# Filler matmuls at the end of routing, the first tiles read by ScalarE, spare tiles that read pads, and three stage changes in a fused state-space, attention and expert kernel

## The chip, the cores and the metric

The kernel runs on one core of one Trainium2 chip. The metric is the device time of one execution in microseconds (us); the time of the kernel before is the median of three runs.

## The reference

Eight batches of 768 tokens with 256 features. The first 256 tokens of a batch (the image) come out of a state-space kernel, the other 512 (the text) are an input. Attention with 16 query and 4 key/value heads of 64 features follows, then a router that sends each token to the 2 best of 8 experts, all in float32:

```
h = tok(log_dt, inv_A_real, A_imag, B_ri, x)         # (8, 256, 256)
h = concatenate([h, txt], axis=1)                    # (8, 768, 256)
h = h + attention(layernorm(h), Wq, Wk, Wv, Wo)      # rotary, softmax, 16 heads on 4
h = h + ffn(layernorm(h), Wr, br, W1, b1, W2, b2)
# ffn: logits = x @ Wr + br; the two largest, softmax over the two;
#      gate * (relu(x @ W1[e] + b1[e]) @ W2[e] + b2[e]), summed over the two experts
```

## The kernel before

There are three blocks of instructions, one after the other; each engine has its own queue in a block and works in order, and semaphores tie the queues together.

**The state-space block** (`vandermonde`) builds powers of a complex number on VectorE, multiplies four banks on TensorE (line 197), lets ScalarE copy each bank out (L171), and stores the image rows of batch 0 to DRAM (L143). The block ends when these stores have landed.

**The attention block** starts with a hand-written order of work for batch 0. SyncE loads the image rows and the text rows of batch 0 (L516, L517) and stores the image rows of the other seven batches (L614). VectorE takes the statistics of all six tiles of 128 tokens (L496, L500), refines the inverse root in small chained instructions (L485 to L504) and normalises four tiles (L850); GpSimd normalises two (L781). TensorE then runs the list `FIRST`: three transposing jobs (L633), four key jobs, four query jobs and four more query jobs for the next group of heads (L642); ScalarE copies each result out of PSUM (L713, L719, L717). VectorE applies the rotary turn to keys and queries in `rotate`, 6 instructions a half (L470, L474, L475). SyncE moves the keys and then, in 16 DMAs, the queries (L622), and the loop over 8 batches and 4 groups of heads begins with the score matmuls (L656) and the maxima (L812).

**The third block** holds `route` and `experts`. In `route`, a batch is six calls of `project` (8 matmuls of 256 columns each, L980), and between them stand, for the batch before, `turn` (12 transposes, L988), `logits` (12 matmuls of 8 columns, L996) and `counts` (L1003, L1004). TensorE's three banks `A[:, t % 3]` are read by VectorE's `add` (L1078). VectorE normalises the batch (`norm`, up to L1103), picks the experts (`choose`, from L1110 to L1125), and gives each pair of token and expert a row (`place`, up to L1149). GpSimd then writes the rows to `xs_d` with 12 indirect DMAs a batch (L963). The last batch has nothing beside it: TensorE's `drain` is `turn`, `logits`, `counts`. After `place`, VectorE writes `tail_i` (L1163), from which SyncE and ScalarE put 128 pad rows behind each expert's rows (L934, L1066), and `tile_table` (L1190 to L1212) works out for each of 103 tiles its expert, the row that it starts at (`src_i`) and for how many earlier output DMAs its own has to wait (`adds_i`). The table has room for more tiles than the data fill. A tile past the last real one reads the last real tile again and has a gate of zero, and `adds_i` makes its output DMA wait for the one before.

In `experts`, SyncE loads the rows and the first weights of four tiles ahead (L1258, L1262). Before the first rows it waits for all scatters, pads and stores. A tile is two transposes (L1292), 8 matmuls up (L1302), a relu on ScalarE (L1340), 4 matmuls down (L1309), bias and gate on VectorE (L1382, L1384), and an indirect DMA on GpSimd that adds the rows to the output in DRAM (L1365); rows with an index beyond the last token are skipped.

## Time and profile before

| what | value |
|---|---|
| time of three runs | 2265.6 to 2272.73 us, median 2267.47 |
| the profiled execution | 2265.04 us, span 2263.3 us |
| busy: TensorE, VectorE, ScalarE, GpSimd | 2047.4, 1770.0, 1072.6, 879.4 us |
| mean granted TensorE clock | 0.959 of 2.4 GHz |

Busy times are sums over the whole span, and the stages have different limits, so the table only says that TensorE is busy for nine tenths of it. What an edit is worth is read from the stage that it touches. The profiled execution spends 1.74 us outside its span and is 2.43 us below the median.

### The profile page before, as it was taken

Reading aid. Unit: us, or ns where it says so; the run is one execution under the profiler, and the core shown is the slowest. Engines: PE = TensorE matmul, PEld = TensorE weight load, DVE = VectorE, ACT = ScalarE, POOL = GpSimd, SP = SyncE. Lnnn points to the kernel's source line nnn. Section 1 sums busy time; section 2 is a strip of 40 time slices with the busy share of each in tenths; the row PEclk is TensorE's granted clock in tenths of the full one; section 3 lists DMA queues with packets and bytes.
Section 4 is the critical chain, followed back from the end, with each engine's and each line's share of the span. In section 5 each row is a group of like instructions: output and inputs, shape, how many; then the busy total and the mean of one; then the engine's idle time right before and its main releaser. Section 6 shows DMA issues by size and latency. Waiting matters only on the chain. (4 is left out here: it accounts for less than half of the span.)

```text
span 2263.3 us, 59177 instructions
## 1 busy us (share of the span) xinstructions
PE 2047.4 (90%) x21098; PEld 1237.6 (55%) x21099; DVE 1770.0 (78%) x3212; ACT 1072.6 (47%) x2463; POOL 879.4 (39%) x833
## 2 busy tenths in 40 slices
PE   0369999999999999999999999997899949999997
PEld 0234444444444444444444445443588839999996
DVE  8769999999999999999999999999144544444443
ACT  2035655655556555655665565555021114444442
POOL 0023454264344542642444436221034443444443
PEclk6689999999999999999999999999899969999998
DMA  2143543634544445435444453453677648898885
GB/s 51 43 107 90 136 118 92 159 106 103 142 113 126 117 107 137 116 108 128 120 120 120 102 133 105 117 131 95 202 258 269 216 136 212 210 212 209 215 210 117
DMA packets 189542, 317.28 MB, mean 140 GB/s; under 512 B 48661, under 2 KB 127121, under 8 KB 189329
## 3 DMA queue, kind: packets, MB, share of 16 engines
q1 hardware_dynamic: 156640, 275.39, 45.1%
q0 software_dynamic: 19440, 25.83, 6.2%
q10 hardware_dynamic: 13248, 13.13, 1.7%
q8 instruction: 144, 2.36, 0.5%
q14 instruction: 70, 0.57, 0.1%
HBM read 214.75 MB, written 92.31 MB: 136 GB/s over the span
## 5 line engine op out<-in xcount | busy, mean ns | idle before, releaser
L725 ACT ACTIVATE a_prob<-ps_s,a_nmax 128x768 f32<-128x768 f32 x768 | 686.3, 898 | 578.9 <-DVE a_nmax L812 578.9
L812 DVE TENSOR_REDUCE a_nmax<-ps_s 128x1 f32<-128x768 f32 x768 | 694.1, 943 | 49.4 <-PE ps_s L656 44.2
L818 DVE STREAM_TRANSPOSE a_probT<-a_prob 128x768 f32<-128x768 f32 x768 | 700.0, 949 | 1.4 <-PE ps_o L663 1.4
L656 PE MATMUL ps_s<-a_kT,a_qT 64*128 64x384 f32 x3072 | 614.7, 514 | 54.7 <-ACT a_prob L725 50.8
L663 PE MATMUL ps_o<-a_probT,a_vrep 32*64 32x384 f32 x12288 | 561.2, 491 | 6.8 <-DVE a_probT L818 5.0
L656 PEld LDWEIGHTS ps_s<-a_kT,a_qT 64*128 64x128 f32 x3072 | 259.7, 186 | 391.5 <-ACT a_prob L725 275.3
L788 POOL TENSOR_TENSOR a_o<-a_o,a_invrow 128x1536 f32<-128x1536 f32 x32 | 110.0, 3437 | 791.0 <-ACT a_o L733 791.0
L663 PEld LDWEIGHTS ps_o<-a_probT,a_vrep 32*64 32x64 f32 x12288 | 243.6, 132 | 293.8 <-issue 129.9
L470 POOL TENSOR_TENSOR a_prod<-a_raw,a_table 128x384 f32<-128x384 f32 x304 | 294.5, 1002 | 29.1 <-DVE a_qp L475 22.1
L1365 POOL DMA_INDIRECT out_dram<-e_y,e_row_i x103 | 160.6, 1559 | 239.9 <-DMA out_dram<-e_y,e_row_i 138.6
L1302 PE MATMUL ps_r<-e_xT,e_w 128*128 128x128 f32 x1648 | 201.8, 276 | 0.0
L1309 PE MATMUL ps_r<-ew,e_hT 128*128 x824 | 194.7, 379 | 0.0
L1302 PEld LDWEIGHTS ps_r<-e_xT,e_w 128*128 128x128 f32 x1648 | 193.3, 193 | 0.1
L1340 ACT ACTIVATE e_hT<-ps_r,e_b_now 128x128 f32<-128x128 f32 x412 | 117.8, 368 | 158.9 <-PE ps_r L1302 100.0
L980 PE MATMUL ps_r<-wo,r_oT 128*128 128x256 f32 x768 | 180.9, 397 | 9.7 <-POOL base L945 9.7
L642 PE MATMUL ps_o<-a_xT,wq 128*128 128x384 f32 x512 | 185.8, 501 | 0.0
L980 PEld LDWEIGHTS ps_r<-wo,r_oT 128*128 128x128 f32 x768 | 151.5, 200 | 32.2 <-POOL base L945 10.4
L1309 PEld LDWEIGHTS ps_r<-ew,e_hT 128*128 128x128 f32 x824 | 148.8, 190 | 16.0
L963 POOL DMA_INDIRECT xs_d<-r_xn,r_idx x96 | 93.8, 977 | 150.1 <-DVE h L1078 119.1
L725 ACT ACTIVATION_READ_ACCUMULATOR a_prob<-ps_s,a_nmax 128x1 f32 x768 | 151.0, 197 | 0.0
L642 PEld LDWEIGHTS ps_o<-a_xT,wq 128*128 128x128 f32 x512 | 91.0, 189 | 88.9 <-issue 25.6
L1382 DVE TENSOR_TENSOR e_y<-ps_r,eb 128x256 f32<-128x256 f32 x103 | 43.7, 424 | 99.9 <-PE ps_r L1309 97.9
(211 smaller groups left out, 1291.5 us busy)
## 6 DMA issues: line engine op xcount, KB each, us to landing
e_w<-in_L_ffn_W_dram SPq DMA_DIRECT2D x103, 512.0 KB, 4.3
a_qT<-q_d SPq DMA_DIRECT2D x124, 384.0 KB, 8.9
a_vrep<-v_d SPq DMA_DIRECT2D x128, 192.0 KB, 3.8
a_invrow<-inv_d SPq DMA_DIRECT2D x64, 384.0 KB, 5.1
oT_d<-a_o SPq DMA_DIRECT2D x32, 768.0 KB, 3.3
r_oT<-oT_d SPq DMA_DIRECT2D x64, 384.0 KB, 8.4
q_d<-a_qp SPq DMA_DIRECT2D x31, 768.0 KB, 3.7
e_x<-xs_d SPq DMA_DIRECT2D x103, 132.0 KB, 3.6
```

What stands on the lines that cost most here:

```text
L470: eng.tensor_tensor(scratch[n], a, f, ALU.mult).then_inc(done, 1)
L642: last = pe.matmul(X[:, 0:HALF], w, xn[:, k, HALF * c:HALF * c + HALF], start=(k == 0), stop=(k == KC - 1))
L656: last = pe.matmul(S[:, s % 2, r, 0:HALF], qT[rows, par, 2 * hp + c, P * t:P * t + P], kT[rows, par, :], start=True, stop=True)
L663: last = pe.matmul(O[DH * c:DH * c + DH, q, 0:HALF], vrep[rows, j % NQ, j // NQ, :], keys(par, c, j, rows), start=(j == 0), stop=(j == NJ ...
L725: act.activation(prob[:, s % RING, :].rearrange("p (r k) -> p r k", r=2), S[:, s % 2, :, 0:HALF], ACT.Exp, bias=nmax[:, s % RING:s % RING ...
L812: v.tensor_reduce(nmax[:, s % RING:s % RING + 1], S[:, s % 2, :, 0:HALF], AX.XY, ALU.max, negate=True).then_inc(max_ready, 1)
L818: v.transpose(turned(par, s), prob[:, s % RING, :]).then_inc(t_ready, 1)
L980: last = pe.matmul(A[:, t % 3, 0:D], oT[:, q, c // 2, c % 2, P * t:P * t + P], wo[:, c, :], start=(c == 0), stop=(c == KV * 2 - 1))
L1302: last = pe.matmul(H[:, q, P * f:P * f + P], w1[:, n, c, P * f:P * f + P], xT[:, q, P * c:P * c + P], start=(c == 0), stop=(c == KC - 1))
L1309: last = pe.matmul(Y[:, q, 0:D], hT[:, q, P * c:P * c + P], w2[:, bass.ds(ex, 1), c, :], start=(c == 0), stop=(c == FC - 1))
L1340: last = act.activation(hT[:, q, P * f:P * f + P], H[:, q, P * f:P * f + P], ACT.Relu, bias=b1_now[:, n, f:f + 1], scale=1.0)
L1365: pool.indirect_dma_start(out=acc_d, out_offset=bass.IndirectOffsetOnAxis(ap=row_i[:, n:n + 1], axis=0), in_=y[:, n, :], in_offset=None, c ...
```

## The change

- **State-space and attention.** The text rows of batch 0 are loaded and normalised within the state-space block (`normalise_rows` on VectorE, after the last of its products). The attention block only loads and normalises the image rows, all on VectorE. `FIRST` starts with the text rows, and the halves of keys and queries that hold only text come first. VectorE's first turns use the buffer `prod`, and they stand before its wait for the stored rows.
- **Routing.** The logits of a batch are put between the matmuls of the third `project` of the next, two matmuls behind each of its last six. TensorE no longer waits for four constants at the start.
- **The end of routing.** `warm(n)` issues n matmuls of 256 columns into a bank that nobody reads; 106 of them are put around the last batch's work and behind it, with waits for `tail_ready` and `table_ready` between.
- **The tile table and the first tiles.** Spare tiles start at the pads behind the last expert's rows, and do not wait for one another. `needs_i` holds for the first 8 tiles whether they need the last batch's rows. ScalarE issues the first four row loads, as soon as the table is there and `placed` has the value that the tile needs; SyncE issues all four first weights at once. GpSimd waits for the stores of the residual before its first output DMA.

```
+def normalise_rows(v, k, x, ln, tiles):
+
+    st, mv, ve, y, y2 = ln
+    some = slice(tiles[0], tiles[-1] + 1)
+    for t in tiles:
+        k.mark(v.bn_stats(st[:, t, :], x[:, t, :]))
+    v.wait_ge(k.sem, k.base + k.n)
+    for t in tiles:
+        k.mark(v.bn_aggr(mv[:, t, :], st[:, t, :]))
+    v.wait_ge(k.sem, k.base + k.n)
+    k.link(v.tensor_scalar(ve[:, some], mv[:, some, 1], EPS, None, ALU.add))
+    k.link(v.tensor_scalar(y[:, some].bitcast(I32), ve[:, some].bitcast(I32), 1, None, ALU.arith_shift_right))
+    k.link(v.tensor_scalar(y[:, some].bitcast(I32), y[:, some].bitcast(I32), -1.0, float(0x5f3759df), ALU.mult, ALU.add))
+    for _ in range(3):
+        k.link(v.tensor_tensor(y2[:, some], y[:, some], y[:, some], ALU.mult))
+        k.link(v.tensor_tensor(y2[:, some], y2[:, some], ve[:, some], ALU.mult))
+        k.link(v.tensor_scalar(y2[:, some], y2[:, some], -0.5, 1.5, ALU.mult, ALU.add))
+        k.link(v.tensor_tensor(y[:, some], y[:, some], y2[:, some], ALU.mult))
+    for t in tiles:
+        last = v.tensor_scalar(x[:, t, :], x[:, t, :], mv[:, t, 0:1], y[:, t:t + 1], ALU.subtract, ALU.mult)
+    return last
+
...
+                sp.dma_start(x0[:, IT:TT, :], io["txt"][0].rearrange("(t p) d -> p t d", p=P)).then_inc(x_in, 16)
...
                     v.wait_ge(g_ready, q + 1)
+                v.wait_ge(x_in, 16)
+                normalise_rows(v, Tally(v, text_dve), x0, ln, range(IT, TT)).then_inc(text_ready, 1)
...
-    FIRST = N_JOBS + K_JOBS + Q_JOBS + Q_JOBS
-    FIRST_AT = {"n": 0, "k": 3, "q": 7, "q1": 11}
+    FIRST = [("text", 0, 0), ("text", 1, 0), ("k", 1, 0), ("k", 1, 1), ("image", 0, 0), ("k", 0, 0), ("k", 0, 1),
+             ("q", 1, 0), ("q", 1, 1), ("q", 0, 0), ("q", 0, 1)] + Q_JOBS
+    IMAGE_AT = FIRST.index(("image", 0, 0))
+    FIRST_AT = {"q1": 11}
...
                 def iteration(b, g):
                     i = b * KV + g
                     if first_it(i):
-                        hold(sp, x_done, len(N_JOBS))
+                        hold(sp, x_done, IMAGE_AT + 1)
...
 
...
                 for c in range(1, NB):
                     sp.dma_start(token_rows(img_d, c), kt[c:P:NB]).then_inc(rows_stored, 16)
-                hold(sp, part["k"], 2 * LINKS)
-                move_k(0, 0)
+                for r in (1, 0):
+                    hold(sp, part["k"], (2 - r) * LINKS)
+                    for h in range(2):
+                        at = DH * r + HH * h
+                        sp.dma_start(kT[at:at + HH, 0, :], kp[0:HH, h, HALF * r:HALF * r + HALF]).then_inc(k_in[0], 16)
...
 
-                    if job == "n":
+                    if job == "text":
+                        for m in range(TT - IT):
+                            last = pe.transpose(X[:, P * m:P * m + P], x[:, IT + m, P * c:P * c + P], ident[:])
+                    elif job == "image":
+                        for m in range(4):
+                            last = pe.transpose(X[:, P * m:P * m + P], x[:, m % IT, P * (m // IT):P * (m // IT) + P], ident[:])
+                    elif job == "n":
...
                     for n in range(NJ // GROUP):
                         group(NB - 1, KV, n)
 
-                pe.wait_ge(norm_ready, 1)
-                pe.wait_ge(norm_first, 1)
+                pe.wait_ge(text_ready, 1)
                 pe.wait_ge(loaded, LOADED)
                 for n, (job, c, h) in enumerate(FIRST):
-                    wait(pe, x_out, len(N_JOBS) if n == len(N_JOBS) else n - NQ + 1)
+                    if n == IMAGE_AT:
+                        pe.wait_ge(norm_ready, 1)
+                    wait(pe, x_out, n if n in (2, IMAGE_AT + 1) else n - NQ + 1)
...
-                    free = (part["q"], (c + 1) * LINKS) if n >= FIRST_AT["q1"] and h == 0 else None
+                    free = (part["q"], (2 - c) * LINKS) if n >= FIRST_AT["q1"] and h == 0 else None
                     evacuate(O[:, n % NQ], n, job, c, h, free)
                 loop(act, iteration, drain)
 
...
 
                 def normalise(n):
-                    if n > 0:
-                        for at in range(3, 6):
-                            stats(pool, n, at)
+                    for at in range(3, 6):
+                        stats(pool, n, at)
                     hold(pool, norm_dve, n * NORMS + NORMS)
-                    for t in range(TT if n else ON_POOL):
+                    for t in range(TT):
                         last = pool.tensor_scalar(x[:, t, :], x[:, t, :], mv[:, t, 0:1], y[:, t:t + 1], ALU.subtract, ALU.mult)
                     last.then_inc(norm_ready, 1)
 
...
                         scale_o(i - 1)
 
-                normalise(0)
...
-                for at in range(6):
-                    stats(v, 0, at)
-                v.wait_ge(norm_dve, NORMS)
-                for t in range(ON_POOL, TT):
-                    last = v.tensor_scalar(x[:, t, :], x[:, t, :], mv[:, t, 0:1], y[:, t:t + 1], ALU.subtract, ALU.mult)
-                last.then_inc(norm_first, 1)
+                v.wait_ge(x_in, 32)
+                k = Tally(v, norm_dve)
+                normalise_rows(v, k, x, ln, range(IT)).then_inc(norm_ready, 1)
+                v.nop().then_inc(norm_dve, NORMS - k.n)
                 v.memset(inv[:], 1.0).then_inc(set_ready, 1)
                 v.wait_ge(set_ready, 1)
                 v.wait_ge(table_in, 16)
+                for job, c, number in (("k", 1, 0), ("k", 0, 1), ("q", 1, 0), ("q", 0, 1)):
+                    rotate(v, job, c, number, [prod[:, n, :] for n in range(4)], FIRST.index((job, c, 1)) + 1, [])
                 v.wait_ge(rows_stored, (NB - 1) * 16)
-                flat = probT[:].rearrange("p a b q -> p (a b q)")
-                for job in "kq":
-                    for c in range(2):
-                        rotate(v, job, c, c, [flat[:, HALF * n:HALF * n + HALF] for n in range(4)], FIRST_AT[job] + 2 * c + 2, [])
                 loop(v, iteration, drain)
 
 
...
                     pool.indirect_dma_start(out=xs_d, out_offset=bass.IndirectOffsetOnAxis(ap=idx[:, q, e, t:t + 1], axis=0),
                                             in_=xn[:, q, t, :], in_offset=None).then_inc(scattered[q], 16)
             pool.wait_ge(scattered[q], k * (TT * TOPK * 16) + TT * TOPK * 16)
-            pool.nop().then_inc(xn_free, 1)
+            if isinstance(b, int) and b >= NB - 2:
+                if b == NB - 1:
+                    for r in range(2):
+                        pool.wait_ge(zeroed[r], 16 * (NE // 2))
+                pool.nop().then_inc(placed, 1)
+            else:
+                pool.nop().then_inc(xn_free, 1)
...
-        def project(b, q, t):
+        def project(b, q, t, beside=None):
             pe.wait_ge(oT_in[2 * q + t // 3], (b >> 1) * (KV * 16) + KV * 16)
             pe.wait_ge(h1_ready, b * TT + t + 1)
             for c in range(KV * 2):
                 last = pe.matmul(A[:, t % 3, 0:D], oT[:, q, c // 2, c % 2, P * t:P * t + P], wo[:, c, :], start=(c == 0), stop=(c == KV * 2 - 1))
+                if beside is not None and c >= KV * 2 - TT:
+                    logits(beside, [c - (KV * 2 - TT)])
             last.then_inc(oT_free, 1)
 
...
-        def logits(b):
-            pe.wait_ge(xT_ready, b * 3 + 3)
-            pe.wait_ge(mask_ready, b + 1)
-            for t in range(TT):
+        def logits(b, tiles):
+            if 0 in tiles:
+                pe.wait_ge(xT_ready, b * 3 + 3)
+                pe.wait_ge(mask_ready, b + 1)
+            for t in tiles:
                 for c in range(KC):
                     last = pe.matmul(L[:, NE * t:NE * t + NE], xT[:, c, P * t:P * t + P], wr[:, c, :], start=(c == 0), stop=(c == KC - 1))
-            last.then_inc(lg_done, 1)
+            if TT - 1 in tiles:
+                last.then_inc(lg_done, 1)
 
         def counts(b):
+            pe.wait_ge(const, 2)
             pe.wait_ge(mask_ready, b + 2)
             pe.wait_ge(idx_ready, b + 1)
...
-                project(b, q, t)
+                project(b, q, t, b - 1 if not first(b) and t == LOGITS_AT else None)
                 if not first(b) and t == TURN_AT:
                     turn(b - 1, 1 - q)
-                if not first(b) and t == LOGITS_AT:
-                    logits(b - 1)
                 if not first(b) and t == COUNTS_AT:
                     counts(b - 1)
 
+        def warm(count):
+            for _ in range(count):
+                pe.matmul(A[:, TT % 3, 0:D], ident[:], wo[:, 0, :], start=True, stop=True)
+
         def drain():
+            pe.wait_ge(h1_ready, NB * TT + 1)
+            warm(26)
             turn(NB - 1, 1)
-            logits(NB - 1)
+            warm(4)
+            logits(NB - 1, range(TT))
+            warm(12)
             counts(NB - 1)
-
-        pe.wait_ge(const, 4)
+            warm(20)
+            pe.wait_ge(tail_ready, 1)
+            warm(32)
+            pe.wait_ge(table_ready, 1)
+            warm(12)
+
         pe.wait_ge(wo_in, 16)
         loop(iteration, drain, pe)
...
             v.tensor_copy(tail_i[:], run[:]).then_inc(tail_ready, 1)
+            k = Tally(v, needs_dve)
+            k.link(v.tensor_scalar(full[:], off[:, 0, 0:1], 1.0 / P, -1.0, ALU.mult, ALU.add))
+            k.link(v.tensor_scalar(needs_i[:], tile_no[:, 0:AHEAD], full[:], 1.0, ALU.is_gt, ALU.add))
             tile_table(v, sb, table_dve, run, base, tile_no, pairs, exp_i, src_i, held_by, adds_i, table_ready).then_inc(adds_ready, 1)
...
     link(v.tensor_copy(end[:, 0:1], cnt[:, 0:1]))
-    for x in range(1, NE):
+    for x in range(1, NE - 1):
         link(v.tensor_tensor(end[:, x:x + 1], end[:, x - 1:x], cnt[:, x:x + 1], ALU.add))
-    link(v.tensor_scalar(last[:], end[:, NE - 1:NE], -1.0, None, ALU.add))
-    link(v.tensor_scalar(jr[:], j[:], last[:], None, ALU.min))
     shape = [P, NT, NE - 1]
-    link(v.tensor_tensor(past[:], jr[:].unsqueeze(2).to_broadcast(shape), end[:, 0:NE - 1].unsqueeze(1).to_broadcast(shape), ALU.is_ge))
+    link(v.tensor_tensor(past[:], j[:].unsqueeze(2).to_broadcast(shape), end[:, 0:NE - 1].unsqueeze(1).to_broadcast(shape), ALU.is_ge))
     link(v.tensor_reduce(e[:], past[:], AX.X, ALU.add))
     link(v.tensor_tensor(past[:], past[:], cnt[:, 0:NE - 1].unsqueeze(1).to_broadcast(shape), ALU.mult))
     link(v.tensor_reduce(start[:], past[:], AX.X, ALU.add))
-    link(v.tensor_tensor(start[:], jr[:], start[:], ALU.subtract))
+    link(v.tensor_tensor(start[:], j[:], start[:], ALU.subtract))
     link(v.tensor_scalar(start[:], start[:], float(P), None, ALU.mult))
     mark(v.tensor_copy(exp_i[:], e[:]))
-    link(v.tensor_scalar(ind[:], j[:], last[:], None, ALU.is_gt))
-    mark(v.scalar_tensor_tensor(out=held_by[:], in0=ind[:], scalar=-2.0 * NE, in1=e[:], op0=ALU.mult, op1=ALU.add))
-    v.scalar_tensor_tensor(out=src_i[:], in0=e[:], scalar=float(STRIDE), in1=start[:], op0=ALU.mult, op1=ALU.add).then_inc(rows_ready, 1)
+    mark(v.tensor_copy(held_by[:], e[:]))
+    link(v.scalar_tensor_tensor(out=start[:], in0=e[:], scalar=float(STRIDE), in1=start[:], op0=ALU.mult, op1=ALU.add))
+    v.tensor_scalar(src_i[:], start[:], run[:, NE - 1:NE], None, ALU.min).then_inc(rows_ready, 1)
     link(v.tensor_tensor(turn[:, 1:NT], e[:, 1:NT], e[:, 0:NT - 1], ALU.is_gt))
-    link(v.tensor_tensor(turn[:, 1:NT], turn[:, 1:NT], ind[:, 1:NT], ALU.max))
     return v.scalar_tensor_tensor(out=adds_i[:, 1:NT], in0=turn[:, 1:NT], scalar=16.0, in1=pairs[:, 1:NT], op0=ALU.mult, op1=ALU.add)
...
         def load(j, n):
+            if isinstance(j, int) and j < AHEAD:
+                needs = sp.value_load(at(needs_i, j), min_val=1, max_val=2)
+                hold(sp, placed, needs)
             row = sp.value_load(at(src_i, j), min_val=0, max_val=SLOTS - P)
             sp.dma_start(x[:, n, :], xs_d[bass.ds(row, P), :]).then_inc(x_in[n], 16)
 
@@ -1261,13 +1321,7 @@
             ex = sp.value_load(at(exp_i, j), min_val=0, max_val=NE - 1)
             sp.dma_start(w1[:, n], io["W1"][bass.ds(ex, 1)].rearrange("o (c p) f -> p (o c) f", p=P)).then_inc(w1_in[n], 16)
 
-        for n in range(2):
-            load_w1(n, n)
-        for s, value in landed:
-            sp.wait_ge(s, value)
         for n in range(RING):
-            load(n, n)
-        for n in range(2, RING):
             load_w1(n, n)
...
@@ -1277,6 +1331,8 @@
                 load(j + RING, n)
                 hold(sp, h_done, j + 1)
                 load_w1(j + RING, n)
+            if isinstance(j, int) and j == AHEAD - RING - 1:
+                sp.wait_ge(placed, 2)
 
...
+        act.wait_ge(table_ready, 1)
+        for n in range(RING):
+            needs = act.value_load(at(needs_i, n), min_val=1, max_val=2)
+            hold(act, placed, needs)
+            row = act.value_load(at(src_i, n), min_val=0, max_val=SLOTS - P)
+            act.dma_start(x[:, n, :], xs_d[bass.ds(row, P), :]).then_inc(x_in[n], 16)
         copy_x(0, 0)
         loop(act, tile)
...
         pool.wait_ge(adds_ready, 1)
+        pool.wait_ge(h_stored, 16 * NB)
         loop(pool, tile)
```

`AHEAD` is 8. `placed` is raised by GpSimd when the scatters of the last batch but one have landed, and again when those of the last batch and all pads have.

## Rows read from the trace of the kernel before

**Rows 1.** The page: span, and the granted clock in 40 slices (tenths).

```profile
span 2263.3 us, 59177 instructions
PEclk6689999999999999999999999999899969999998
```

**Rows 2.** Timeline, VectorE around the first block border: start, duration, instruction, idle before.

```profile
108.94 2.06 DVE L496 BATCH_NORM_STATS2 a_st<-a_x 128x6 f32<-128x256 f32 x6 [15.88 <-DMA a_x<-in_txt_dram]
...
111.58 0.17 DVE L502 TENSOR_SCALAR a_ve<-a_mv 128x6 f32<-128x6 f32 x1
...
114.75 1.61 DVE L850 TENSOR_SCALAR a_x<-a_x,a_mv,a_y 128x256 f32<-128x256 f32 x4
...
127.15 1.96 DVE L470 TENSOR_TENSOR a_probT<-a_raw,a_table 128x384 f32<-128x384 f32 x4 [10.75 <-ACT a_raw L719]
...
138.81 0.55 DVE L475 TENSOR_TENSOR a_qp<-a_probT 128x384 f32<-128x384 f32 x1
```

**Rows 3.** Timeline, SyncE's queue: loads of batch 0, moves of its queries.

```profile
104.54 0.38 SPq L516 DMA_DIRECT2D a_x<-img_d  x1
...
139.43 10.97 SPq L622 DMA_DIRECT2D a_qT<-a_qp  x16
```

**Rows 4.** DMA issues, 100 to 145 us: size and median us to landing.

```profile
a_x<-img_d SPq DMA_DIRECT2D x1, 256.0 KB, 2.7
```

**Rows 5.** Timeline, ScalarE's copies of the first two key jobs.

```profile
123.97 0.49 ACT L719 ACTIVATE a_raw<-ps_o 128x384 f32<-128x384 f32 x1 [3.02 <-PE ps_o L642]
126.53 0.49 ACT L719 ACTIVATE a_raw<-ps_o 128x384 f32<-128x384 f32 x1 [2.07 <-PE ps_o L642]
```

**Rows 6.** Timeline, TensorE's first transposes and first scores.

```profile
117.50 2.82 PE L633 MATMUL ps_o<-ident,a_x 128*128 128x128 f32 x12 [17.04 <-POOL a_x L781]
...
143.54 2.66 PE L656 MATMUL ps_s<-a_kT,a_qT 64*128 64x384 f32 x8 [3.94 <-DMA a_qT<-a_qp]
```

**Rows 7.** The chain of waits, two batches of routing: start, duration, piece.

```profile
1672.45 2.58 PE ps_r L996 x24
1675.03 3.56 PE ps_r L980 x16
...
1694.16 3.46 PE ps_r L980 x16
...
1700.19 5.24 PE ps_r L980 x16
```

**Rows 8.** Stretches: length; busy PE, PEld, DVE, ACT, POOL; granted clock; DMA.

```profile
1700.00:1705.00 5.00, 5.00 (x17) 4.13 (x17) 2.42 (x24) 1.49 (x2) 0.96 (x1) 0.66 1.10 372
...
1855.00:1860.00 5.00, 0.00 (x0) 0.00 (x0) 0.00 (x0) 0.00 (x0) 0.96 (x1) 0.50 0.23 78
```

**Rows 9.** Timeline, the last batch's routing and the first tile.

```profile
1824.24 2.82 PE L988 MATMUL ps_r<-ident,r_xn 128*128 128x128 f32 x12 [5.75 <-DVE r_xn L1103]
...
1833.07 0.21 DVE L1110 TENSOR_TENSOR r_lg<-ps_r,br 128x48 f32<-128x48 f32 x1 [8.89 <-PE ps_r L996]
...
1835.77 0.67 PE L1003 MATMUL ps_r<-r_mask,r_below 128*128 128x48 f32 x2 [2.74 <-DVE r_mask L1124]
...
1839.17 0.17 DVE L1149 CAST r_idx<-r_posf 128x12 uint32<-128x12 f32 x1
...
1847.53 0.26 DVE L1209 SCALAR_TENSOR_TENSOR src_i<-t_e,t_start 128x103 int32<-128x103 f32 x1
...
1860.62 0.69 PE L1292 MATMUL ps_r<-ident,e_x 128*128 128x128 f32 x2 [23.76 <-DMA e_x<-xs_d]
...
1868.88 1.95 PE L1302 MATMUL ps_r<-e_xT,e_w 128*128 128x128 f32 x16
```

**Rows 10.** Timeline, the last output DMAs and the last tile's result.

```profile
2236.76 1.55 POOL L1365 DMA_INDIRECT out_dram<-e_y,e_row_i  x1 [2.05 <-DVE e_y L1384]
...
2248.16 0.35 DVE L1384 TENSOR_SCALAR e_y<-e_y,e_gate 128x256 f32<-128x256 f32 x1
...
2255.17 1.55 POOL L1365 DMA_INDIRECT out_dram<-e_y,e_row_i  x1 [2.98 <-DMA out_dram<-e_y,e_row_i]
```

More of the change, by code:

```diff
@@ L1184, in tile_table @@
     ni = sb("t_ni", [P, NE], I32)
[L1185 to L1186 removed]
+    e, start, turn = (sb(f"t_{x}", [P, NT]) for x in ("e", "start", "turn"))
     past = sb("t_past", [P, NT, NE - 1])
```

47 lines of the change are left out of this document (27 added, 20 removed).

## The prediction

> **What bounds the kernel now.** I read the page first. Its row of the granted clock is full almost everywhere, and the slices below it are the first three, slice 29, where routing starts, and slice 33, where routing ends [rows 1]. In between lies the attention loop, about 1,450 us of a fixed pipeline. No part of the change touches it, so what is gained ahead of it arrives whole at the end. Next I read the timeline at three places that the diff touches. At the first block border VectorE is idle for 15.88 us for the text rows, and the queries' moves start only when its last rotary turn has ended [rows 2, 3]. In routing the chain of waits runs on TensorE alone. At the end of routing TensorE waits for everybody, at a granted clock of 0.50 [rows 8, 9]. In the expert loop TensorE is the bound again, and at the very end GpSimd's output DMAs are [rows 10].
>
> **Part 1, start of attention.** The text rows' statistics and four normalised tiles move into VectorE's idle time behind its last product. That is 2.06 us of statistics and 1.61 us of scaling for at least as many tiles, with some 3.2 us of small instructions between, under 7 us in 15.88 us of idle time, and the block border before the image load at 104.54 comes after it [rows 2, 3]. It costs nothing; without that cover it would be 7 us. The image rows land 2.7 us after 104.54, at 107.2 [rows 3, 4]. VectorE then needs two tiles of six (0.7 us of statistics, 0.2 of aggregation), the same small chain of 3.17 us (111.58 to 114.75), and two scalings (0.8): ready at 112.2, where TensorE began at 117.50 [rows 2, 6]. TensorE has transposed the text by 107.2 and done both key jobs of the second half by 112.3, at 2.56 us a job on the low clock [rows 5]. The image's transposes and copy take some 1.6 us more, to 113.9. The next two key jobs end at 116.5 if the clock has risen (half of 2.56 each) and at 119.0 if not, and are copied 0.7 us later. From there VectorE has three rotary turns of 3.05 us in a row (the four before run from 127.15 to 139.36) [rows 2]. They end at 126.4 or 128.9, in place of 139.36. That is 13.0 or 10.4 us; I take 12, because TensorE has by then worked for 7 us with one pause. What stands behind it, the moves of the queries and 4 us later the first scores, follows at the same distance [rows 3, 6]. GpSimd loses its two tiles. The first turns now use `prod`, which GpSimd takes over only after both query turns, as before. The seven stores of image rows are issued from the same time on.
>
> **Part 2, logits between the project's matmuls.** The matmuls are the same. A pass of a logit matmul is as long as its weight load (2.58 us for 24), a project pass as long as its 256 columns (3.46 us for 16) [rows 7]. The order does not change that sum, so the interleaving by itself is worth nothing. But behind five of seven logit stretches the next project takes 5.24 us in place of 3.56, and the clock over that stretch is 0.66 [rows 7, 8]. It fell after 2.58 us in which only 8 columns followed each weight load. With a project matmul before each pair, no such stretch is left. If the clock then holds, five times 1.68 is 8.4 us. VectorE's add of the third tile comes 2.3 us later and delays the choice of experts by some 0.5 us; the next to need it is `counts` behind the fourth project, which has about that much slack. The price is between 0 and 1 us in all; I take 0, and bound the gain at 0 and 8.4. The constants that TensorE no longer waits for I count at nothing, since the block border holds it too.
>
> **Part 3, the end of routing.** A filler is a float32 matmul of 256 columns with a weight load, the shape of a project matmul. Eight of these are 16 records in 3.46 us, so one is two passes and 0.433 us [rows 7]. The 106 fillers therefore hold TensorE for 45.9 us at the full clock. Before, from the end of the projects (1824.24 less 5.75, 1818.49) to the first tile's transposes at 1860.62 were 42.1 us [rows 9]. The fillers do not give way, so I add up TensorE's queue:
> 26 fillers, 11.2 us, to 1829.7 (the normalised batch has been there since 1824.2);
> `turn` 1.45 us (half of its 2.82 and a little), 4 fillers 1.7, `logits` 2.58, to 1835.5;
> 12 fillers, 5.2, to 1840.7 (the mask is ready 2.7 us after the logits, at 1838.2);
> `counts` 0.4, to 1841.1; the indices came 3.57 us after it started, some 3.1 on the full clock, so at 1843.8, where it was 1839.34 [rows 9].
> Then 20, 32 and 12 fillers, 27.7 us, to 1868.8. Neither wait holds them. `tail_ready` comes at 1843.8, and the table, 8.45 us from index to `src_i` before, has two instructions of 0.2 us more and six fewer, 7.7 us in sum, to 1851.5. ScalarE's row loads need about 1.5 us to issue and 2.7 to 4.3 to land, by 1857; even behind the whole old chain of scatters and pads, shifted by 4.5 us, they would be there by 1865.2. So the first transposes start at 1868.8, not at 1860.62: 8.2 us late. The full clock in the first tiles gives some 1.6 us back (0.69 us of transposes and a first tile's matmuls at half speed; bounds 0 and 2.5). The sum of this part is a loss of 6.6 us. The loads by ScalarE, the early weights and the shorter table are hidden behind the fillers. The wait for stores ahead of GpSimd's first output DMA is met long before its first tile, and SyncE's two more register loads a tile lie in a ring of four tiles.
> The Trainium skill (TensorE: Matmul & The Clock Gate, Back-to-back issue gap) gives 262 cycles for a matmul of 256 columns, 0.109 us at 2.4 GHz. By it the fillers would be 11.6 us and no delay at all. This case's row has four times that for float32, and the row decides.
>
> **Part 4, spare tiles.** The last four output DMAs each wait for the one before: from 2236.76 to 2255.17 is four steps of 4.60 us, while the last tile's result was there at 2248.5 [rows 10]. Now a DMA waits for the one two before it. The last can issue at about 2249.8 (0.95 us after its result, or 1.9 us after its neighbour), 5.4 us earlier. A DMA whose rows are all skipped may land sooner; nothing shows it, and it can give between 0 and the 3.7 us to landing. I take 0.
>
> **The sum.** 12.0 + 8.4 + 5.4 - 6.6 is 19.2 us. From the span of 2263.3 that is 2244.1; with the 1.74 us around it, 2245.8. The median of the runs lies 2.4 us above the profiled execution, so 2248 us against 2267.47.
>
> **The rivals.**
> *The clock still falls (18%).* Transposes and logits remain short streams, and a few low stretches stay or move. For it: the clock fell five times of seven here [rows 7, 8]. Against: the project's long passes now stand in every microsecond of it. All 8.4 us lost gives 2257.
> *The start doesn't matter (10%).* Something with a time of its own, such as the stores of the other seven batches, holds the first scores or the first loop. Against: the scores follow the moves by 4 us and end the wait [rows 3, 6]. The 12 us gone gives 2260; this part would then not do what it says.
> *Fillers are cheap (10%).* If a filler is one pass, 0.216 us, the 106 are 22.9 us. The turn is not delayed, the logits come at 1830.0, the table at 1843, the rows at 1847.8, and the first transposes some 12.8 us earlier than before, with the 1.6 us a gain of 14.4. That gives 2227. Against it stand 16 records for 8 matmuls. The page named above speaks for it.
> *Slower (5%).* The fillers run on the low clock. Each then costs 0.865 us, another 45.9 us for all of them: 2294. The batch before ends at the full clock and nothing idles between, which speaks against it. It decides for slower once 60 of the 106 are slow (26 us over 0.433).
>
> **How the numbers follow.** The forecast has the remaining 57%. Its own range is 2242 to 2254: 10.4 to 13 us at the start, 6.7 to 8.4 of clock, 4.5 to 7.5 at the end, a loss of 5 to 8 in the middle. The range takes in the first two rivals and leaves out cheap and slow fillers, 15%: 2238 to 2261. A change under 0.3% (6.8 us) is about what a measurement of this kernel cannot tell from none. The slow fillers are slower (5%), the upper ends of the first two rivals lie within 0.3% (5%), and all else, 90%, is faster.
>
> **What would show it.** First scores at 131 to 134 us. Project pieces behind the logits of 3.5 us, and no slice at 0.66 in routing. Fillers with two records each and 0.43 us; the last batch's turn some 11 us after its projects; no idle time of TensorE before the first tile's transposes, 50 us after the projects, with rows in place 10 us earlier. Output DMAs at the end 3.7 us apart or less. The forecast fails if fillers are not two passes, if the clock is not held, or if the first loop waits for something else.

## The result, and the profile after

The changed kernel took 2275.82 us (median of 20 runs, 2265.15 to 2291.12), the kernel before 2266.15 us (20 runs, 2262.59 to 2272.73): a ratio of 1.0045, 95% interval 1.003 to 1.006. It was slower by 9.7 us where 2248 was forecast. The profiled execution of it is the longest of the 20, so its rows overstate the typical run; but they show where the time is. One of the six runs of `fillers_fit` below (4234.83 us) and one of the eleven of before beside it (2502.28 us) were in a slow state; the medians include them, the ratios leave them out. The page, span and granted clock, for [rows 1]:

```profile
span 2289.3 us, 59644 instructions
PEclk6579999999999999999999999998978999999999
```

Timeline of the changed kernel, VectorE and TensorE at the start, for [rows 2, 6] (start, duration, instruction, idle before):

```profile
98.16 1.38 DVE L94 TENSOR_SCALAR a_x<-a_x,a_mv,a_y 128x256 f32<-128x256 f32 x4
107.88 0.75 DVE L80 BATCH_NORM_STATS2 a_st<-a_x 128x6 f32<-128x256 f32 x2 [8.34 <-DMA a_x<-img_d]
...
131.61 2.93 PE L693 MATMUL ps_s<-a_kT,a_qT 64*128 64x384 f32 x8 [3.64 <-DMA a_qT<-a_qp]
```

The text rows are normalised in idle time, and the first scores start at 131.61 where they started at 143.54 [rows 6]: 11.9 us, as forecast. Now the middle of routing, a stretch for which [rows 7] showed 3.56 us of project behind a block of logits. Timeline of one batch:

```profile
1687.81 0.40 ACTq L1100 DMA_DIRECT2D out_dram<-h  x1
...
1692.23 1.47 PE L1033 MATMUL ps_r<-ident,r_xn 128*128 128x128 f32 x12
...
1695.27 0.60 ACT L1092 ACTIVATE r_xT<-ps_r 128x512 f32<-128x512 f32 x1 [7.49 <-remote]
...
1696.90 0.52 PEld L1042 LDWEIGHTS ps_r<-wr,r_xT 128*128 128x128 f32 x4 [2.30 <-ACT r_xT L1092]
1696.90 0.61 PE L1042 MATMUL ps_r<-wr,r_xT 128*128 128x8 f32 x4 [1.90 <-ACT r_xT L1092]
...
1698.22 0.86 PE L1042 MATMUL ps_r<-wr,r_xT 128*128 128x8 f32 x4
```

The turn's twelve transposes run from 1692.23 to 1693.70. ScalarE's first copy needs four of them, and starts 0.64 us after the first where nothing is late (1631.52 for 1630.88, an earlier batch); here it starts 3.04 us after it. Its releaser is "remote": the semaphore rose at that moment, but no recorded instruction ended near it. TensorE has by then issued three of the eight matmuls of the next project and stands before the first piece of logits with the project unfinished: its matmuls are idle for 1.9 us, its weight loads (PEld) for 2.3. Then it goes on at the lower clock. Stretches (length; busy PE, PEld, DVE, ACT, POOL; granted clock; DMA share and GB/s) of the changed kernel: behind the first two of its stops, and all of routing:

```profile
1663.00:1672.00 9.00, 9.00 (x35) 8.10 (x35) 0.46 (x2) 1.28 (x1) 0.00 (x0) 0.52 0.83 274
1697.00:1706.00 9.00, 9.00 (x35) 8.10 (x36) 0.60 (x2) 1.15 (x1) 1.45 (x2) 0.53 1.01 344
...
1601.00:1834.50 233.50, 221.93 (x1047) 194.99 (x1048) 95.01 (x514) 33.40 (x50) 73.39 (x85) 0.90 0.63 210
```

This happens in five of seven batches. The view of waits over routing (us in total, times, longest) counts them:

```profile
ACT r_xT L1092 <- remote: 31.9, 6, 7.7
DVE h L1136 <- remote: 16.5, 4, 4.3
...
PE ps_r L1042 <- ACT r_xT L1092: 11.5, 5, 3.9
```

Here "DVE h" is VectorE's add behind a project: it too is told late that TensorE is done. A signal of TensorE that rises over 1 us after the work it tells of is called a late signal from here on. From first to last project routing takes 233.9 us (1601.06 to 1834.97) where it took 207.5 (1610.97 to 1818.49). The end of routing, for [rows 9]:

```profile
1834.81 11.39 PE L1064 MATMUL ps_r<-wo,ident 128*128 128x256 f32 x52
1846.04 1.04 PE L1033 MATMUL ps_r<-ident,r_xn 128*128 128x128 f32 x8
1848.01 0.27 PE L1033 MATMUL ps_r<-ident,r_xn 128*128 128x128 f32 x1 [0.94 <-issue]
...
1851.46 2.74 PE L1042 MATMUL ps_r<-wr,r_xT 128*128 128x8 f32 x24
```

26 fillers are 52 records in 11.2 us, two passes and 0.43 us each, as forecast. The turn breaks off twice, for 0.94 and 1.13 us, with nothing on record that it waits for ("issue"), and the first expert transposes start at 1893.77, 58.8 us after the last project, where 50.4 was forecast and 42.1 measured before.

### The profile page after: what moved, and what is told of

Same layout as the page of the kernel before. It is cut to its first block and busy times, and to the rows that moved or that the text cites. A ratio compares the mean times of both kernels' runs of the same rounds, so it can differ in the third digit from the quotient of the medians.

```text
span 2289.3 us, 59644 instructions
## 1 busy us (share of the span) xinstructions
PE 2115.1 (92%) x21310; PEld 1290.2 (56%) x21311; DVE 1772.8 (77%) x3227; ACT 1073.0 (47%) x2463; POOL 876.3 (38%) x831
## 5 line engine op out<-in xcount | busy, mean ns | idle before, releaser
L693 PE MATMUL ps_s<-a_kT,a_qT 64*128 64x384 f32 x3072 | 623.0, 520 | 49.8 <-ACT a_prob L767 46.2
L1023 PE MATMUL ps_r<-wo,r_oT 128*128 128x256 f32 x768 | 197.1, 411 | 9.0 <-DVEq L1227 9.0
```

Source lines behind the costliest of these rows:

```text
L693: last = pe.matmul(S[:, s % 2, r, 0:HALF], qT[rows, par, 2 * hp + c, P * t:P * t + P], kT[rows, par, :], start=True, stop=True)
L1023: last = pe.matmul(A[:, t % 3, 0:D], oT[:, q, c // 2, c % 2, P * t:P * t + P], wo[:, c, :], start=(c == 0), stop=(c == KV * 2 - 1))
```

## Experiments

Each kernel's time is a median of 4 to 10 runs beside runs of before on the same chip; kernels of one group ran on one chip. "after" below is the changed kernel.

**Group 1: undo each half.** Theory A: the interleaved logits stop TensorE; theory B: something else of the change makes the signals late; rival: the fillers pay for themselves.

`plain_logits`, after with
```
-                project(b, q, t, b - 1 if not first(b) and t == LOGITS_AT else None)
+                project(b, q, t)
...
+                if not first(b) and t == LOGITS_AT:
+                    logits(b - 1, range(TT))
```


> The changed kernel with the six pieces of logits put back behind the third project of their batch; everything else of the change stays. Theory A (the interleaved logits are what stops TensorE: a piece needs ScalarE's copies 2.2 us earlier than the block did, so copies that come 2 to 5 us late hold a half-done project and the clock falls): first project to last project takes about 207.5 us again instead of 233.9, no project beside logits above 3.6 us, and the time is 2275.8 less what the stalls cost in a typical run, about 2266 (start -10, end of routing +15, spare tiles -5.6). Theory B (something else of the change makes TensorE's signals come late in batches 2 to 6, and the interleaving only shows it): ScalarE's r_xT copies are still about 2.4 us late in the trace, and routing stays above 215 us.

`no_fillers`, after with
```
-            for _ in range(count):
+            for _ in range(0):
```


> The changed kernel without its 106 filler multiplications; the waits between them stay. Theory A: from the last project to the first up product it is again about 50 us instead of 65.6 (TensorE waits at the lower clock, as before), so about 15 us less than the change: near 2261. Rival (the fillers pay for themselves by the clock they hold): the first tiles run slower without them and the time stays within 4 us of 2275.8. The late copies of batches 2 to 6 stay as they are by both.

`neither`, both edits.


> The changed kernel with neither the interleaved logits nor the fillers: only the start of attention, the tile table with its spare tiles and ScalarE's first rows are left of the change. If the pieces add up: -10 from the start, -5.6 from the spare tiles, nothing in routing, 2266 - 16 = about 2250. If start and spare tiles give back their gain elsewhere (a theory that the profiled pair alone can't exclude), 2258 to 2266.

`before_beside`, the kernel before with the interleaving alone:
```
                 last = pe.matmul(A[:, t % 3, 0:D], ...)
+                if beside is not None and c >= KV * 2 - TT:
+                    logits(beside, [c - (KV * 2 - TT)])
```


> The kernel before with one edit: the logits in six pieces inside the third project. Theory A: copies late in some batches, TensorE idle before L996's pieces, routing 5 to 26 us longer than 207.5, time 2268 to 2290 and a wider spread of runs than before's 10 us. Theory B (the lateness comes from another part of the change): the clock is held in the batches, routing is 199 to 207 us, time 2258 to 2266.

Measured, with before at 2264.67: plain_logits 2254.22 (ratio 0.9952, 0.9938 to 0.9965), no_fillers 2234.23 (0.9859, 0.9844 to 0.9874), neither 2241.96 (0.9902, 0.9887 to 0.9917), before_beside 2255.37 (0.9964, 0.9952 to 0.9977). None of the four traces has a late copy, though two are interleaved. So theory A as I put it fell: the interleaving alone wins 9.3 us in one kernel and 7.7 in the other (2234.2 for 2242.0), and routing is 199.2 and 199.5 us with it, 207.7 and 207.8 without. The rival fell too: fillers cost 12.3 us (2254.2 for 2242.0). The kernel `neither` came 8 us below its expectation, because the first transposes start 34.2 us behind the projects without fillers, not 42.1 as before; the expectation had left the early row loads and the shorter table at nothing. The parts add up to 2246.5 for the changed kernel, and it had taken 2275.8.

**Group 2: the same kernel again, and the fillers.** `after_again` is the changed kernel word for word; the other three change only the counts of fillers in `drain`, which were 26, 4, 12, 20, 32, 12: `fillers_fit` 12, 2, 6, 5, 17, 11; `first_only` 26 and then none; `last_only` none, none, none, 20, 32, 12. The counts of `fillers_fit` come from the idle time in the trace of no_fillers (timeline):

```profile
1803.91 2.79 PE L1033 MATMUL ps_r<-ident,r_xn 128*128 128x128 f32 x12 [5.84 <-DVE r_xn L1161]
...
1815.46 0.63 PE L1051 MATMUL ps_r<-r_mask,r_below 128*128 128x48 f32 x2 [2.79 <-issue]
...
1832.15 0.69 PE L1348 MATMUL ps_r<-ident,e_x 128*128 128x128 f32 x2 [15.63 <-DMA e_x<-xs_d]
```

> The changed kernel once more, word for word, on the chip that times the other three of this group. Both halves of the change can be undone without a late copy in any trace: logits behind the project 2254.2, no fillers 2234.2, neither 2242.0. Theory C (the late copies of batches 2 to 6 are a property of this program, of both edits together): the r_xT copies are late again in 5 batches, routing above 215 us, time 2265 to 2291. Theory D (they belong to the chip or the hour of those runs, and not to the kernel): no late copy, routing about 199.5 us, time about 2234.2 + 12.3 (what the fillers cost without interleaving) = 2246.5.

> The changed kernel with 53 fillers for 106, each group cut to the idle stretch that the trace without fillers shows: 12 ahead of the turn (5.84 us idle), 2, 6 (2.79 us), 5, 17 and 11 (together 16 us). Theory A (fillers are late only where they outlast the wait; the clock that they hold is worth some us in the first tiles): last project to first expert transposes about 33 us, tail 396 to 398 us instead of 401.6: 2229 to 2232. Rival (the clock is worth nothing, or the fillers disturb the signals by being there at all): 2234 or more, with late copies in routing if theory C holds for fewer fillers too.

> The changed kernel with only the 26 fillers ahead of the last turn. They take 11.2 us where TensorE waited 5.8 us: +5.4 us at that place, less 1.4 + 2.6 us that the turn and the logits win at the full clock; time about 2234.2 + 1.5 = 2236 if nothing else moves, 2240 where the clock has fallen again before the logits end.

> The changed kernel with only the 64 fillers behind the counts (20, 32 and 12). 64 x 0.433 us = 27.7 us where TensorE waited 16.0 us without them: +11.7 us at the full clock, more at the lower one in which they begin, and 4 to 6 us back in the tail: 2240 to 2246. If late copies in routing come from fillers at the end, they would show here too and the time would be 2260 or more.

Measured, before at 2266.05: after_again **2246.61** (0.9913, 0.99 to 0.9926), fillers_fit 2230.91 (0.9842, 0.9829 to 0.9855), first_only 2235.97 (0.9875, 0.986 to 0.9889), last_only 2243.81 (0.9903, 0.9888 to 0.9918). The same program as the changed kernel, 29 us faster. The fillers cost what they were expected to: 2236 was forecast for first_only, 2240 to 2246 for last_only, and no late signal is in either trace. In the trace of after_again TensorE runs through routing without a stop at a clock of 0.99 (stretch), no wait of ScalarE has "remote" (waits), and a piece follows the third step of its project (chain):

```profile
1600.00:1797.50 197.50, 197.50 (x1045) 176.49 (x1045) 95.35 (x514) 33.07 (x50) 71.40 (x75) 0.99 0.74 247
```

```profile
ACT r_xT L1092 <- PE ps_r L1033: 30.6, 6, 5.2
```

```profile
1654.77 1.30 PE ps_r L1023 x6
1656.07 0.34 PE ps_r L1042 x4
1656.41 0.53 PE ps_r L1023 x2
```

Its end (timeline), with the fillers behind the counts in one row of 64, and the last two output DMAs for [rows 10]:

```profile
1808.59 1.47 PE L1033 MATMUL ps_r<-ident,r_xn 128*128 128x128 f32 x12
...
1821.55 27.86 PE L1064 MATMUL ps_r<-wo,ident 128*128 128x256 f32 x128
1831.72 0.27 DVE L1267 TENSOR_SCALAR src_i<-t_start,run 128x103 int32<-128x103 f32 x1
...
1849.25 0.60 PE L1348 MATMUL ps_r<-ident,e_x 128*128 128x128 f32 x4
...
2235.06 1.56 POOL L1427 DMA_INDIRECT out_dram<-e_y,e_row_i  x1 [2.15 <-DMA out_dram<-e_y,e_row_i]
...
2236.93 1.55 POOL L1427 DMA_INDIRECT out_dram<-e_y,e_row_i  x1 [0.30 <-issue]
```

The table is ready at 1831.99 and TensorE multiplies on for 17 us. Late signals, then, are not a property of this program alone; theory D stands. Theory C fell.

**Group 3: another chip.**


> The changed kernel a third time, word for word. On the chip of the second time it took 2246.6 us with no late copy (routing 199.7 us), where the first time it took 2275.8 with late copies in five batches. Theory D1 (the late signals belong to one chip): 2246 us here if this is another chip without them, 2265 to 2291 if it is the one with them, and then for the kernel without fillers of this group too. Theory D2 (they come with the hour, whatever the chip): either, with no link to the chip.

> The changed kernel without fillers once more, beside the changed kernel on one chip: 12 to 13 us below it where neither is disturbed (2234 for 2246). Where the changed kernel shows late copies, this one tells whether fillers have a part in them: without a part it is disturbed as well (2255 to 2265), with one it stays at 2234.

Measured, before at 2266.05: after_third 2269.28 (1.0016, 1.0001 to 1.0031), no_fillers_again 2252.28 (0.9937, 0.9917 to 0.9957). Both traces have late signals; the copies are late in three and in four of the seven batches, and routing is 219.8 and 217.9 us. The kernel without fillers loses 18 us too (2252.3 for 2234.2), so fillers are not what makes signals late. It is also still 14 us faster than before, with its interleaved logits: in such a session it takes the late signals and the fillers together (17 us between the two kernels here) to use up the gain.

**Groups 4 to 6: does before have late signals, and does slack help?** `before_traced`, `before_traced_b` and `before_traced_c` are the kernel before, for its trace; `plain_again` and `before_beside_again` are those of group 1. `slack`, `slack_b` and `slack_c` are fillers_fit with
```
-    TURN_AT, LOGITS_AT, COUNTS_AT = 1, 2, 3
+    TURN_AT, LOGITS_AT, COUNTS_AT = 1, 3, 4
...
-                    paced = (b + 1) * TT + COUNTS_AT + 4 + t
+                    paced = (b + 1) * TT + 7 + t
```


> The kernel before, word for word, for a trace of it on the chip of this group. Theory E (late signals are a property of some chips under full transfers, and before only hides them, since its logits need the copies a whole project later): on a chip where before_beside_again has late copies, this trace has them too, TensorE does not wait for them, routing is 207.5 us. Theory F (the interleaving makes them): no late copy here on any chip.

> The changed kernel with its logits behind the third project. 2254 us on a chip without late signals. On one with them: theory E 2254 to 2258 (late copies in the trace, but no idle time before the logits), theory F 2254 with no late copy at all; if signals late by 1 to 3 us cost time by themselves, wherever the logits stand, 2265 or more.

> The kernel before with only the interleaved logits. 2255 us on a chip without late signals; on one with them 2270 to 2285, routing 215 to 230 us, by theories E and F alike. It says of which kind the chip of this group is.

> The changed kernel with 53 fillers as in fillers_fit, and the logits' pieces inside the fourth project of their batch instead of the third (counts and the choice behind them one project later too). A piece now needs the copies 3.45 us later. Theory E: late signals of up to 3.3 us stop TensorE no more, routing about 199.5 us on either kind of chip, time about 2231. Rival: the choice and the scatters come one project later, and the next batch's rows wait for them: routing 205 us or more.

Measured, before at 2264.16: before_traced 2263.87, plain_again 2251.67 (0.9943, 0.9925 to 0.9962), before_beside_again 2256.72 (0.9969, 0.9957 to 0.998), slack 2230.23 (0.9848, 0.9815 to 0.988). No late signal in any of the four; only the rival of slack is answered: routing 199.6 us, the later choice costs nothing.

> The kernel before once more, for a trace on another chip. Theory E: on a chip where the other kernel of this group has late signals, so has this one, and routing stays 207.5 us. Theory F: none here on any chip.

> The kernel slack once more. Without late signals 2230 us. With late signals of 1 to 3.3 us: 2230 to 2233 if a project of slack hides them (theory E), 2248 or more if they cost time wherever the pieces stand.

Measured, before at 2264.7: before_traced_b 2264.52, slack_b 2230.01 (0.9851, 0.9835 to 0.9868). Again no late signal.

> The kernel before a third time, for a trace on another chip. Theory E: late signals where slack_c has them, routing 207.5 us all the same. Theory F: none here on any chip.

> The kernel slack a third time. Without late signals 2230 us; with them 2230 to 2233 by theory E, 2248 or more if they cost time wherever the pieces stand.

Measured, before at 2266.29: before_traced_c 2265.36 (0.9994, 0.9984 to 1.0004), slack_c **2263.97** (1.0, 0.9985 to 1.0015). Late signals in both traces. The kernel before, waits over routing and timeline of one batch:

```profile
DVE h L1078 <- remote: 12.9, 5, 4.0
DVE r_lg L1110 <- remote: 11.0, 3, 4.0
...
ACT r_xT L1034 <- remote: 7.5, 1, 7.5
...
PE ps_r L1003 <- DVE r_mask L1124: 2.7, 3, 1.4
```

```profile
1668.72 1.47 PE L988 MATMUL ps_r<-ident,r_xn 128*128 128x128 f32 x12
...
1671.76 0.60 ACT L1034 ACTIVATE r_xT<-ps_r 128x512 f32<-128x512 f32 x1 [7.50 <-remote]
...
1672.73 0.61 ACT L1034 ACTIVATE r_xT<-ps_r 128x512 f32<-128x512 f32 x1
1673.39 2.75 PEld L996 LDWEIGHTS ps_r<-wr,r_xT 128*128 128x128 f32 x24
```

The copy starts 3.04 us after the transposes, the same as in the changed kernel. But here a whole project lies between the turn and the block of logits. The last copy ends at 1673.34 and the block's weights load at 1673.39, with no idle time before them. The first copy is late in three of the seven batches, by 2.2 to 2.4 us, and TensorE waits for none of them; routing is 207.5 us as ever. Not all of that is hiding. The logits' result is told late too (`r_lg`), the choice comes later, and TensorE waits 2.7 us in three batches before `counts` (L1003). Its mean granted clock over 1613 to 1818 us is 0.97 here and 0.95 in the profile before, and that gives the time back. So the first half of theory E, that late signals cost before nothing, holds in this trace, in part by luck. Its other half, that a project of slack does the same for the changed kernel, fell. The kernel slack, waits and timeline of one batch:

```profile
ACT r_xT L1092 <- remote: 63.4, 9, 10.6
...
DVE h L1136 <- remote: 36.0, 6, 7.2
```

```profile
1653.46 1.47 PE L1033 MATMUL ps_r<-ident,r_xn 128*128 128x128 f32 x12
1658.26 0.60 ACT L1092 ACTIVATE r_xT<-ps_r 128x512 f32<-128x512 f32 x1 [9.26 <-remote]
1660.41 0.60 ACT L1092 ACTIVATE r_xT<-ps_r 128x512 f32<-128x512 f32 x1 [1.55 <-remote]
1662.53 0.60 ACT L1092 ACTIVATE r_xT<-ps_r 128x512 f32<-128x512 f32 x1 [1.52 <-remote]
1663.17 0.52 PEld L1042 LDWEIGHTS ps_r<-wr,r_xT 128*128 128x128 f32 x4 [3.89 <-ACT r_xT L1092]
```

The lateness is no fixed 2.4 us that a longer slack could cover: in six batches the first copy is 4.2 to 5.6 us late, and in the batch above the third is 7.6 us late. The adds are late too. TensorE waits for copies in only three batches, 5.3 us in all. But in four batches it also stops inside the third project, where no instruction of the program waits:

```profile
1719.53 0.38 PE L1023 MATMUL ps_r<-wo,r_oT 128*128 128x256 f32 x1 [0.84 <-issue]
1720.26 1.78 PE L1023 MATMUL ps_r<-wo,r_oT 128*128 128x256 f32 x7 [0.35 <-issue]
```

It goes on at 1720.26, and the batch's first copy starts 0.1 us later. Routing took 217.5 us for 199.6 without late signals, and the way from there to the first transposes 8.0 us more.

## Why the prediction was wrong

It was right of the kernel without late signals, and wrong of the runs that it was measured by. Against after_again (span 2244.8 for 2263.3, 18.5 us less; forecast 19.2):

| term | forecast | measured in after_again | by |
|---|---|---|---|
| Part 1, first project of routing | -12.0 | -13.1 | 1597.9 for 1611.0 |
| Part 2, first to last project | -8.4 | -7.8 | 199.7 for 207.5 |
| Part 3, last project to first transposes | +8.2 | +9.6 | 51.7 for 42.1 |
| Parts 3 and 4, from there to the end | -1.6 - 5.4 | -7.2 | 395.5 for 402.7 |

**Part 1** holds. Fourteen traces with the new start begin routing at 1598.2 on average, six with the old one at 1610.2. In the profiled run of the result it was 9.9 us: its first scores came 2.2 us later than in after_again, and the first iteration ran at a granted clock of 0.50 throughout (stretch 144 to 158 us) where after_again had 0.72.

**Part 2** is the step that failed, and not in the size of its gain: before_beside gives 9.3 us for a forecast of 8.4, of which 8.3 us lie in the routing of its trace (199.2 for 207.5). In the profile of the result the same term is a loss of 26.4 us. The prediction wrote "The price is between 0 and 1 us in all; I take 0", and that price is what failed. It looked for what is late next only on VectorE ("delays the choice of experts by some 0.5 us") and took the order of TensorE's work as free. It did not ask how early a piece of logits needs ScalarE's copies. In a batch without late signals the last copy ends 0.4 us before the first piece (1633.10 and 1633.49 in the profile after), where before it ended 2.5 us ahead of the block (1642.89 and 1645.44). With signals 2.4 us late, before_traced_c shows no stop at the logits, the changed kernel's trace shows one inside a project, then the lower clock for some 7 to 14 us, five times. Over 1601 to 1834.5 us TensorE is idle for 11.6 us and busy for 221.9, where all of routing takes 199.7 in after_again: two thirds of the difference is the lower clock. That the lost slack is the cause is argued from these traces and not shown: slack_c has a project more of it and lost 18 us in routing all the same, with signals later than in any other run, and neither before_beside nor plain_logits was run where signals are late. Shown is that the loss comes and goes with the late signals while the program stays the same. The profiled pair differs by 26.0 us: 9.9 less at the start, 26.4 more in routing, 16.7 more to the first transposes (58.8 for 42.1), 7.2 less behind them. The typical run is 29 us slower than in the session without late signals (2275.8 for 2246.6); the two traces, of 2289.3 and 2244.8 us, differ by 3.2 us at the start, 34.2 in routing and 7.1 from there to the first transposes. The rival "the clock still falls" had the symptom, with another cause and a third of the price (8.4 us): it gave back what was won, while a stop costs time that before never lost.

**Part 3** is right: 0.43 us a filler, 51.7 us for 50.4. What the text called hidden is real: without fillers the first transposes come 34.1 us after the projects, not 42.1, because of ScalarE's early row loads and the shorter table. The fillers cover this 8 us and add 9.6. They give back 2.4 us behind the first up product (394.6 us to the end for 397.0 without them), near the forecast 1.6. In sum they cost 12.3 us against the same kernel without them. The forecast's 6.6 was against before, where TensorE waited 8 us longer than it now would; it did not ask what the kernel would be without fillers. The rivals of cheap and of slow fillers fell. (Two sums of the prediction are 1 us off: 8.4 us above 2248 is 2256, not 2257, and the low end of its range comes to 2243, not 2242.) Fillers cut to the idle time lose nothing and win perhaps 3 us (2230.9 for 2234.2, on two chips, intervals that overlap).

**Part 4** is 0.6 to 1.3 us short of its forecast: from the first up product to the end 396.3 and 397.0 us without fillers for 401.1, so 4.1 to 4.8 us for a forecast of 5.4, and the last two output DMAs 1.9 us apart instead of 4.6.

**What stays open: what holds TensorE's signals back.** They mostly come as a burst. The trace's semaphore events put the three banks of the batch shown above at 1695.25, 1695.31 and 1695.37, where the work ends, by its records, at 1692.83, 1693.27 and 1693.70. That looks like work that was done and told late. But the first late batch of the same trace has them at 1659.33, 1660.77 and 1662.23, and that of slack_c 2.1 us apart (1658.24, 1660.38, 1662.50). In four later batches of slack_c TensorE itself stands still and goes on 0.1 to 0.8 us before they rise, as it does in the turn of the last batch above. So whether only the telling is late, or TensorE is held too, is not settled. It is no property of one chip (theory D1 fell, D2 stands): the group of after_again and the sixth group ran on the same one, by its number on record. The late signals seen are all TensorE's; in the batch shown above ScalarE's signals match its records (1695.88 for a copy that ends at 1695.87). In routing they lie where the DMA share is near 1.0, but a few come late among the last batch's fillers too, at a share of 0.19 (stretch 1846 to 1850 of the changed kernel), so full transfers alone don't explain them. Two more things bear on it. Records of DMA landings are missing there (DMA issues, 1640 to 1690: first the changed kernel with late signals, then after_again without; count, KB, median us to landing):

```profile
r_oT<-oT_d SPq DMA_DIRECT2D x15, 384.0 KB
out_dram<-h ACTq DMA_DIRECT2D x2, 768.0 KB
```

```profile
r_oT<-oT_d SPq DMA_DIRECT2D x16, 384.0 KB, 6.0
out_dram<-h ACTq DMA_DIRECT2D x2, 768.0 KB, 12.6
```

No median can be given where landings are lost. Counted over whole traces, the five with late signals hold 17,130 to 17,554 records of landings and the other fifteen 20,198 to 20,230, for the same DMAs; up to 1640 us all twenty hold 12,238 to 12,432. The records go missing from the stretch on in which the first signals come late, in the kernel before as well. In the expert loop they are missing without loss of time: 394.6 us from the first up product to the end in the profiles after and after_again. So late signals and lost records come together in every trace; which brings the other is not shown, but it points to the path on which events are recorded. The Trainium skill (NOTIFIC — the notification-queue block, 7.1 Overflow: three behaviours, one of which stalls the engine) says that the recording block's internal pipeline holds up the producer rather than lose a record. The trace agrees only in part: TensorE's pauses fit it, and records were lost all the same. No run here shows that this is it, and all runs are recorded alike, so none without recording was there to compare. Instruction fetch, my first suspect, is out. From 1690 to 1730, with two late batches, the changed kernel's DMA queues were these alone:

```profile
q1 hardware_dynamic: 4476, 5.39, 41.0%
q10 hardware_dynamic: 2315, 2.32, 16.4%
q0 software_dynamic: 752, 2.14, 13.9%
```

No instruction packet is among them; the 50 us ahead have five, in the kernel before as in this one. The Trainium skill (Runtime: NRT & Kernel Launch, Instruction fetch mechanics) tells of a stall where a branch leaves the loaded pages; that would need such packets. Whether plain logits with the new start keep their 2252 to 2254 us when signals are late was not run. The medians in us, by what the traces show:

| kernel | no late signals | late signals |
|---|---|---|
| before | 2263.9, 2264.5 | 2265.4 |
| after | 2246.6 | 2275.8, 2269.3 |
| no fillers | 2234.2 | 2252.3 |
| fit fillers, logits a project later | 2230.2, 2230.0 | 2264.0 |

## What to carry over

A reordering that costs no engine any work can still spend slack. Before moving an instruction ahead, take the time from its operand's last write to its own start, before and after the move; with copies 2.4 us late, the kernel with 2.5 us of slack did not wait for them and the one with 0.4 us stopped five times, and each stop was followed by the lower clock. Slack is no insurance by itself: with a project more of it, slack_c lost 34 us to signals that came later still. Work put in to fill a wait must be sized by the wait that is left after the other edits (16 us here, filled with 28), or it becomes the wait: without its fillers the kernel was faster than before in both kinds of session (2234.2 and 2252.3 us). And a change that rests on timing between engines should be run in several sessions: one program took 2246.6 and 2275.8 us here, while the one it is compared with stayed within 3 us.

## What was unexpected of the hardware

TensorE's semaphore signals can reach the other engines 1 to 7.6 us after the work is done, often three of them 0.06 us apart in a burst, in some sessions and not in others on the same chip. VectorE's adds and ScalarE's copies showed it, in all four programs that were traced in such a session, and in all five of those traces some 2,700 to 3,100 of 20,200 records of DMA landings are missing. The delays differ by program: up to 7.6 us in slack_c, up to 2.9 in the kernel before, both traced in one session. What makes them differ is open.
